# An attention and mixture-of-experts block on one core: the last ten tiles' residual, LayerNorm 2 steps and low rows on VectorE, the last six tiles' router work in three PSUM banks

## The reference

```
h = layernorm(x) * (1 + ca) + sa
x = x + ga * attention(h)        # 16 heads, 16 segments of 64 tokens, causal inside a segment,
                                 # a memory M, z per head carried from segment to segment
h = layernorm(x) * (1 + cb) + sb
logits = h @ router_w.T          # 8 experts, 2 per token
x = x + gb * (weighted sum of the two chosen experts' silu(gate) * up @ w2)
```

## Time and profile before

| | us |
|---|---|
| median of three runs | 1365.4 |
| lowest and highest of them | 1361.44 and 1370.28 |
| the profiled execution | 1369.37 |
| its span, first to last instruction | 1367.3 |
| DVE busy in it | 939.0 (69%) |
| POOL busy | 927.2 (68%) |
| PE busy | 1192.2 (87%) |
| ACT busy | 706.6 (52%) |

### The profile page before, as it was taken

One profiled execution on the slowest core, in us unless ns is written; L12 is line 12 of the kernel. 1 busy time (PEld: TensorE's weight loads), 2 busy tenths in 40 slices (PEclk: granted clock), 3 DMA queues, 4 the chain that ended last, 5 costly groups with the idle time before them and its releaser, 6 DMA issues. The chain is left out here.

```text
span 1367.3 us, 54718 instructions
## 1 busy us (share of the span) xinstructions
PE 1192.2 (87%) x20142; PEld 1016.3 (74%) x20142; DVE 939.0 (69%) x2509; ACT 706.6 (52%) x1391; POOL 927.2 (68%) x989
## 2 busy tenths in 40 slices
PE   3499999999889998989613899999999999999995
PEld 0277778787767777767413699999999999999994
DVE  2389889998888998878668655555555555555552
ACT  2267878887878887877632222323322232322321
POOL 3158989998988898888910466666666666666643
PEclk8599999999999999999855999999999999999998
DMA  9811333334443434443461454545455455555540
GB/s 225 175 55 51 76 91 94 91 96 109 110 97 88 104 104 99 109 99 97 112 216 16 105 99 91 98 92 98 91 101 101 92 95 95 98 94 98 99 75 1
DMA packets 124476, 134.54 MB, mean 98 GB/s; under 512 B 26090, under 2 KB 103986, under 8 KB 124098
## 3 DMA queue, kind: packets, MB, share of 16 engines
q0 software_dynamic: 32592, 56.77, 22.0%
q1 hardware_dynamic: 89762, 67.46, 20.1%
q10 hardware_dynamic: 1872, 6.82, 1.8%
HBM read 63.60 MB, written 44.04 MB: 79 GB/s over the span
## 5 line engine op out<-in xcount | busy, mean ns | idle before, releaser
L1131 PE MATMUL psum<-xT,xall 128*128 128x256 f16 x3408 | 396.6, 273 | 2.5 <-DVE xT L1118 0.9
L1131 PEld LDWEIGHTS psum<-xT,xall 128*128 x3408 | 331.1, 98 | 40.9 <-issue 3.2
L1191 POOL DMA_INDIRECT out<-yo,sidx x142 | 226.4, 1594 | 198.4 <-DVE yo L1182 172.1
L1139 ACT ACTIVATE sg<-psum 128x512 f32<-128x512 f32 x142 | 84.7, 597 | 317.6 <-PE psum L1131 282.8
L1144 DVE SCALAR_TENSOR_TENSOR hf<-psum,sg 128x512 f32<-128x512 f32 x142 | 98.2, 691 | 209.2 <-ACT sg L1139 205.3
L1101 POOL DMA_INDIRECT grow<-moe_rows,gidx x142 | 142.6, 1004 | 99.5 <-DVE sidx L992 56.5
L1165 PE MATMUL psum<-w2s,hT 128*128 x1704 | 197.7, 273 | 2.6 <-DVE w2s L1217 2.4
L1165 PEld LDWEIGHTS psum<-w2s,hT 128*128 128x128 f16 x1704 | 166.5, 98 | 22.5 <-issue 3.2
L1151 ACT ACTIVATE hT<-hf 128x512 f16<-128x512 f32 x142 | 89.5, 630 | 111.4 <-DVE hf L1144 104.6
L569 POOL TENSOR_TENSOR pT<-sc,pT 128x1024 f16<-128x1024 f32 x64 | 136.5, 2133 | 10.1 <-ACT pT L565 10.1
L1155 DVE TENSOR_TENSOR hT<-hf,hT 128x512 f16<-128x512 f32 x142 | 98.3, 692 | 57.0 <-ACT hT L1151 40.4
(11 more groups left out here) (217 smaller groups left out, 2429.9 us busy)
## 6 DMA issues: line engine op xcount, KB each, us to landing
stk<-qk SPq DMA_DIRECT2D x384, 64.0 KB
moe_rows<-hrows SPq DMA_DIRECT2D x128, 128.0 KB, 2.4
out<-xall SPq DMA_DIRECT2D x128, 64.0 KB, 2.1
xall<-in_x SPq DMA_DIRECT2D x8, 896.0 KB, 18.1
raw<-in_w ACTq DMA_DIRECT2D x13, 512.0 KB, 5.5
raw<-in_w SPq DMA_DIRECT2D x8, 512.0 KB, 7.9
grow<-moe_rows,gidx POOLq DMA_INDIRECT x142
out<-yo,sidx POOLq DMA_INDIRECT x142
```

Source lines behind the costliest of these rows:

```text
L1131: i = k.e.matmul(bank[:, n * LONG:(n + 1) * LONG], w13s[:, bass.ds(ex_reg * (G * 4 * I) + ((2 * c + b_) * 2 * I + col), P)], xT[:, k.b, a, ...
L1139: done(k.e.activation(sg[:, half, :], bGate[half][:, :], ACT.Silu, scale=1.0 / W_SCALE), "sg")
L1191: k.e.indirect_dma_start(out_rows, bass.IndirectOffsetOnAxis(ap=sidx[:, n:n + 1], axis=0), yo[:, k.v, q, :], None, bounds_check=B * T - 1, ...
```

## The change

The four elementwise stages `res_add`, `ln2_mult`, `ln2_add` and `rows_lo` run on VectorE, instead of on GpSimd, for tiles 54 to 63 (LATE = 54). They have semaphores of their own, and `when` directs whoever waits for such a tile to them. For tiles 58 to 63 (END = 58) the router's transposes alternate between bank C (odd tiles) and bank H (even tiles), and the logits go to bank B. Banks B and C are otherwise used by the projections and by `update`, so these tiles also wait until `update_dve` of the last tile is done.

```
+LATE = NT - 10
+END = NT - 6
...
-    bkAh, bkDh, bkHh = bkA.bitcast(F16), bkD.bitcast(F16), bkH.bitcast(F16)
+    bkAh, bkCh, bkDh, bkHh = [bank.bitcast(F16) for bank in (bkA, bkC, bkD, bkH)]
...
+    LATE_ON_VECTOR = ("res", "l2a", "l2b", "hlo")
+    S_late = {n: sem("a_late_" + n) for n in LATE_ON_VECTOR}
...
+            if of >= LATE and stage in LATE_ON_VECTOR:
+                return S_late[stage], of - LATE + 1
...
+    def done_late(ins, stage):
+        ins.then_inc(S_late[stage], 1)
...
     def res_add(k):
-        k.wait("gat")
-        done(k.e.tensor_tensor(k.of_tile(xall), k.of_tile(xall), gat[:, k.b, :], ALU.add), "res")
+        if k.t < LATE:
+            k.wait("gat")
+            done(k.e.tensor_tensor(k.of_tile(xall), k.of_tile(xall), gat[:, k.b, :], ALU.add), "res")
+    def res_add_late(k):
+        if k.t >= LATE:
+            k.wait("gat")
+            done_late(k.e.tensor_tensor(k.of_tile(xall), k.of_tile(xall), gat[:, k.b, :], ALU.add), "res")
...
     def ln2_mult(k):
-        k.wait("xn2")
-        done(k.e.tensor_tensor(h2[:, k.b, :], h2[:, k.b, :], mods[:, mCB, k.j, :], ALU.mult), "l2a")
+        if k.t < LATE:
+            k.wait("xn2")
+            done(k.e.tensor_tensor(h2[:, k.b, :], h2[:, k.b, :], mods[:, mCB, k.j, :], ALU.mult), "l2a")
     def ln2_add(k):
-        k.wait("l2a")
-        done(k.e.tensor_tensor(h2[:, k.b, :], h2[:, k.b, :], mods[:, mB2, k.j, :], ALU.add), "l2b")
+        if k.t < LATE:
+            k.wait("l2a")
+            done(k.e.tensor_tensor(h2[:, k.b, :], h2[:, k.b, :], mods[:, mB2, k.j, :], ALU.add), "l2b")
...
+    def ln2_mult_late(k):
+        if k.t >= LATE:
+            k.wait("xn2")
+            done_late(k.e.tensor_tensor(h2[:, k.b, :], h2[:, k.b, :], mods[:, mCB, k.j, :], ALU.mult), "l2a")
+    def ln2_add_late(k):
+        if k.t >= LATE:
+            k.wait("l2a")
+            done_late(k.e.tensor_tensor(h2[:, k.b, :], h2[:, k.b, :], mods[:, mB2, k.j, :], ALU.add), "l2b")
...
     def rows_lo(k):
-        k.wait("hhi")
-        done(k.e.tensor_tensor(hrows[:, k.j, D:2 * D], h2[:, k.b, :], hrows[:, k.j, 0:D], ALU.subtract), "hlo")
+        if k.t < LATE:
+            k.wait("hhi")
+            done(k.e.tensor_tensor(hrows[:, k.j, D:2 * D], h2[:, k.b, :], hrows[:, k.j, 0:D], ALU.subtract), "hlo")
+    def rows_lo_late(k):
+        if k.t >= LATE:
+            k.wait("hhi")
+            done_late(k.e.tensor_tensor(hrows[:, k.j, D:2 * D], h2[:, k.b, :], hrows[:, k.j, 0:D], ALU.subtract), "hlo")
...
+    def h2_bank(k):
+        return bkCh if k.t >= END and k.t % 2 else bkHh
     def h2_trans(k):
         k.wait("hhi")
         k.wait("hlo")
-        k.wait_banks("h2Tr")
+        if h2_bank(k) is bkCh:
+            k.e.wait_ge(S["umul"], NT)
+            k.wait("h2T", 2)
+        elif k.t >= END + 2:
+            k.wait("h2T", 2)
+            k.wait("gat", -4)
+        else:
+            k.wait_banks("h2Tr")
         for n in range(2 * G):
-            i = k.e.transpose(bkHh[:, n * P:(n + 1) * P], hrows[:, k.j, n * P:(n + 1) * P], idh[:, :])
+            i = k.e.transpose(h2_bank(k)[:, n * P:(n + 1) * P], hrows[:, k.j, n * P:(n + 1) * P], idh[:, :])
...
         k.wait("rtr", 2)
-        done(k.e.activation(h2T[:, k.b, :, :, :].rearrange("p a c t -> p (a c t)"), bkHh[:, 0:2 * D], ACT.Copy), "h2T")
+        done(k.e.activation(h2T[:, k.b, :, :, :].rearrange("p a c t -> p (a c t)"), h2_bank(k)[:, 0:2 * D], ACT.Copy), "h2T")
+    def logit_bank(k):
+        return bkB if k.t >= END else bkH
     def router(k):
         k.wait("h2T")
-        k.wait_banks("rtr")
+        if k.t >= END:
+            k.e.wait_ge(S["umul"], NT)
+            k.wait("lg", 1)
+        else:
+            k.wait_banks("rtr")
         for c in range(G):
             for a, b_ in PARTS:
-                i = k.e.matmul(bkH[:, D:D + E], h2T[:, k.b, a, c, :], rws[:, b_, c, :],
+                i = k.e.matmul(logit_bank(k)[:, D:D + E], h2T[:, k.b, a, c, :], rws[:, b_, c, :],
                                start=(c == 0 and (a, b_) == PARTS[0]), stop=(c == G - 1 and (a, b_) == PARTS[-1]))
         done(i, "rtr")
     def logit_copy(k):
         k.wait("rtr")
-        done(k.e.activation(logits[:, :, k.t], bkH[:, D:D + E], ACT.Copy,
+        done(k.e.activation(logits[:, :, k.t], logit_bank(k)[:, D:D + E], ACT.Copy,
                                scale=1.0 / W_SCALE), "lg")
...
         "vector": [(2, aggr), (9, mem_a), (9, mem_v), (0, stats), (9, v_rest), (9, v_new), (11, pv_den),
-                  (11, pv_scale), (11, pv_dve), (14, ln2_shift), (8, q_rest), (8, sigma), (13, resid),
-                  (9, row_max), (10, update_dve), (13, stats2), (7, h1t_rest), (8, mem_den), (9, max_rest),
-                  (13, aggr2), (8, mem_rec), (13, var_eps2)],
+                  (11, pv_scale), (11, pv_dve), (14, ln2_shift), (16, rows_lo_late), (8, q_rest), (8, sigma), (13, resid),
+                  (9, row_max), (10, update_dve), (13, res_add_late), (13, stats2), (7, h1t_rest), (8, mem_den), (9, max_rest),
+                  (13, aggr2), (8, mem_rec), (13, var_eps2),
+                  (15, ln2_mult_late), (15, ln2_add_late)],
```

## The result

| | before | changed kernel |
|---|---|---|
| median of 20 runs each, us | 1361.98 | 1372.23 |
| lowest and highest | 1355.77, 1370.28 | 1366.46, 1381.80 |
| span of the profiled execution | 1367.3 | 1373.0 |
| `resid` of tile 54 to the next block, in the profile | 86.46 | 98.07 |

The ratio is 1.0071, with a 95% interval from 1.0051 to 1.009: slower, by less than 1%. The three runs shown ahead of the prediction had a median 3.4 us above that of all 20, so 1372 against 1362 is the pair to compare: +10.3 us where the sum said +12.0.

The account below looks back on a forecast made before the run. VectorE and GpSimd were taken as full first, GpSimd alone from tile 60. Delays of 12.5 us at tile 63 less 0.55 gave +12.0 on 1369.4, 1381.3; less 4.0 to the median, 1377 us, range 1362 to 1386.

Parts of the forecast that it names:

- the sum: Attention stage: 12.5 us delay at `resid` of tile 63 less 0.55 in the stage's end gives +12.0 us.
- the relief rival: Tiles 60 to 63: taking 2.8 us a round off full POOL (GpSimd) pays first; -4 us, 1361, chance 0.13.
- VectorE sets the pace: Up to tile 60: moved instructions add 1.6 us a round of own time, plus waits; `resid` of tile 60 +9.7 us.
- Turns: Moved two-SBUF-input instructions on VectorE wait for GpSimd's running instruction: 1.35 us a round, from 0 to 2.5.
- The stall at `v_rest`: VectorE waits for ScalarE's `v_high`, queued behind `rows_hi`, which waits for the LayerNorm pair: 0.6 us, tiles 56 and 57.
- Tile 59 to 60: Stretch between these residuals: 3.0 us added less 2.2 us that VectorE was free; running delay from +8.9 to +9.7.
- The clock: Stretches from tile 58 on: TensorE's clock falls earlier, slowing `pv`, `scores`, `w_o`; +18 us, 1383; clock and more 0.17.
- The ring: From tile 60 on: chain from `resid` over VectorE's pair, ScalarE and `w_o` to the next `resid`, 6.2 us.
- Tile 60 to 61: Stretch of 7.67 us before: 6.2 us plus 1.2 for the pair meeting `p_rest` of tile 63, 7.4, so -0.3.
- No turns: Moved 128x256 instructions on VectorE do not wait for POOL: about 7.5 us less, +4.5, 1370, chance 0.20.
- The tail: From `resid` of tile 63 to the next block: stores end it, 13.3 us against 13.85, -0.55.
- the bank edit itself I cost at 0: Stage's end: the three banks' gain is covered by the stores; without that cover it would bring 2.6 us.

Follow-up runs that it names:

- the one-operand kernel: Changed kernel with each of the four late instructions replaced by statistics over one SBUF tile, against the kernel before: ratio 1.0041 (1.0005 to 1.0077).
- the banks-only kernel: Kernel before with the three banks alone, all four elementwise steps staying on GpSimd: ratio 0.9998, 1363.31 us.
- the two from tile 60 on: Changed kernel with the four steps on VectorE for tiles 60 to 63 only, in its own or the early VectorE order, against before: 1.0024 and 0.9987.
- the early places: Changed kernel with low rows, pair and residual earlier in VectorE's list, against before: 1.0091 for all ten tiles, 0.9987 for the last four.

## Why the prediction was right, step by step

The direction, the mechanism and the size were right, but the closeness of the sum is in part luck. By the table, the sum and the profile differ by 0.4 us at the stage's end and by up to 1.15 us in single stretches, with both signs: the stretches of tiles 56 to 58 were taken 0.8 and 1.1 us too long, those of tiles 59 to 61 1.15 and 1.0 too short. The range was 24 us wide and held "no change" (1365.4), so lying in it says little; and 1361, the price of the relief rival, lies outside it, against what the prediction says of its lower end.

*VectorE sets the pace (right).* Stretch of tile 56 to 57: own work 1.6, turns 0.40 + 0.50 (residual and low rows, by their durations), stall 0.62, less the 0.3 that VectorE was free: 2.8, measured 2.76 (11.17 - 8.41). Stretch of 57 to 58: 1.6 + 0.28 + 0.58 less the 1.76 of the wait for `scores` and 0.3: 0.4, measured 0.40. Stretch of 58 to 59: 1.6 + 1.0 + 0.5, less 0.25 as the weight rounding no longer waits (1.22 at 659.34, for the 1.47 of the earlier trace rows) and 0.25 of VectorE's gaps: 2.6, measured 2.60. The own times and the stall hold, with the turns put in as they came; the prediction itself left out the 0.3 us that VectorE was free in the first of these stretches.

*Turns (right in kind, too large).* The prediction took 0.6 for the residual, 0.3 for the pair and 0.45 for the low rows, 1.35 a round, and 1.2 at the last `p_rest`: 7.9 us over five rounds (it wrote "about 7.5"). The ten tiles show 0.5 on average for the first six residuals (0.94 for that of tile 55, most of why tile 56 is late by 1.6 and not 1.1), nothing for the pair but the 1.17 at `p_rest` of tile 63, and 0.5, 0.28, 0.5 and 0 for the low rows: 5.2 us in their durations, 4.4 at the stage's end by the one-operand kernel. The step that was mis-sized is "for the pair 0.3, near half of a 0.7 instruction": at the end of VectorE's round GpSimd is idle and waits for VectorE's own `var_eps2`, since the moved work is what used to fill it (idle 1.29, 2.22 and 1.95 us there, then the inverse root, in the rounds of tiles 56 to 58).

*The stall at `v_rest` (right).* Predicted 0.6, measured 0.62 and 0.58, and gone in every kernel in which the pair isn't at the end of these rounds.

*Tile 59 to 60 (wrong, and it evened the sum out).* Predicted +0.8, measured +1.95 (8.90 - 6.95), with 2.2 us of VectorE idle: not VectorE's doing. TensorE's clock was 0.73. The banks-only kernel has 8.68 us there at 0.68, the two from tile 60 on 8.34 at 0.71 and 9.01 at 0.51. In the profile of before the clock fell a stretch later; all nine experiments and the changed kernel show it by this stretch (0.51 to 0.73). Part of it comes back in the next stretch (6.97 for 7.67 in the banks-only kernel), and at tile 63 that kernel is 1.3 us late. So I estimate that about 1.3 us of the measured 11.6 belong to the one profile of before and not to the change; 10.3 are left, and the medians differ by 10.3. A second profile of before would show it, and there is none.

*The clock (the rival, +18).* Half of its mechanism came: the clock fell to 0.66 for tiles 58 to 59. Its price didn't: VectorE, not TensorE, was last there, and the 2.60 us of that stretch are accounted for without it. In this profile it costs where VectorE has room, in one stretch.

*The ring (right, 0.25 to 0.55 long).* Predicted 6.2, measured 5.96 and 5.65. The 0.3 for turns of the pair is again what was too much, and in the second `a_high` has no tile left, for which the 5.96 have 0.31 (685.41 to 685.72). Tile 60 to 61 was predicted at 7.4 and took 8.40; the meeting with the last `p_rest` was as taken (1.17 for 1.2). The rest stands in ScalarE's timeline of the changed kernel:

```profile
677.71 0.42 ACT L772 ACTIVATE hrows<-h 128x256 f16<-128x256 f32 x1 [2.41 <-DVE h L767]
...
678.50 1.05 ACT L69 ACTIVATE xall<-raw 128x1024 f16<-128x1024 f32 x1
...
679.45 0.41 ACT L691 ACTIVATE ah<-att_o 128x256 f16<-128x256 f32 x1
679.75 0.59 ACT L707 ACTIVATE aT<-psum 128x512 f16<-128x512 f16 x1
```

The weight rounding `w13_high` (L69) of this round stands between `rows_hi` and `a_act`, 2.04 us from start to start where the ring above has 1.11. And `update_dve` stands once more between `resid` and the residual: 2.12 us from `resid` to the pair for 1.80. So 5.96 + 1.17 + 0.93 + 0.32 = 8.38 of the 8.40; the prediction had both instructions at nothing here.

*POOL's relief (the rival on the other side, -4).* Out: GpSimd's list did get short, but no stretch between residuals did. The ring over VectorE and ScalarE is 5.7 to 6.0, where the rival needed under 4.7. Its premise, which the sum shares ("here POOL was the bound"), fails too for the last two stretches. Busy time by stretch with the early places, tiles 61 to 62 for all ten tiles and 62 to 63 for the last four:

```profile
673.16:677.98 4.82, 2.77 (x20) 1.75 (x20) 4.39 (x11) 2.50 (x6) 2.10 (x2) 0.50 0.11 26
...
677.90:682.42 4.52, 2.78 (x20) 1.76 (x20) 2.92 (x11) 2.14 (x5) 0.66 (x1) 0.50 0.30 65
```

GpSimd is busy 2.10 and 0.66 us there, for 4.82 and 4.06 in the earlier trace rows, and the stretches are 4.82 and 4.52 all the same. In the shorter one the chain over TensorE and ScalarE stands at the same offsets in both kernels: `router`, `logit_copy`, `h2_trans`, `h2_act`, `a_act` and `w_o` start 0.53, 0.86, 1.25, 1.87, 2.37 and 3.02 us behind `resid` of tile 62 in before, and 0.52, 0.86, 1.25, 1.88, 2.37 and 3.02 here. In the longer one, with `a_high` in it, the offsets agree within 0.01 us as well (`w_o` at 3.32 in both). That chain, not GpSimd, sets those rounds.

*No turns (+4.5).* Out by the rows above. The one-operand kernel, which is that rival made real, lost 7.2 us in the stage, 5.9 without the 1.3 of the clock: by that estimate the rival's own price was 1.4 too low.

*The tail (right in sum, wrong in its cause).* Predicted 13.3, measured 13.19. But the step "the bank edit itself I cost at 0: it is covered by the stores" failed: in before the logits, not the stores, were last, by 0.8 us, and behind the moved instructions they would have been later still. The edit alone brings 0.8 us, with the moved instructions 1.8. The last issue's end came 11.17 us behind `resid`, for 11.6, and the block's end 2.02 behind that, for 1.7.

## What to carry to other kernels

In these traces, moving elementwise work with two SBUF inputs from GpSimd to VectorE cost its own time on VectorE plus the wait behind whatever GpSimd was in at that place, however short the moved instruction was; look up, for each place in the list, what GpSimd runs then, the longest instruction above all. GpSimd being full is no reason to relieve it: for six of the ten tiles VectorE was as full, and in the last rounds another chain set the pace. And where a moved step releases a third engine, write the ring out, step by step, with every instruction that stands in it in that round: it gave the new length within 0.25 to 0.55 us where that was done, and was 1.0 short where two instructions were left out.

## What was not expected of the hardware

TensorE's granted clock falls near the end of the attention stage, and in kernels with the same instructions up to tile 60 it doesn't fall in the same stretch: from tile 59 to 60 it is 1.00 in before, 0.68 with only the bank edit, 0.71 and 0.51 in the two kernels that move from tile 60 on, and in these last two it is 0.89 and 0.92 already one stretch earlier. From 6.95 to 8.68 us this stretch moves by 1.7, more than the whole effect of the bank edit. It shows why one profile's stretches must be held against a second kernel that is equal up to there.

A VectorE addition of eight columns took 1.52 us, over nine times its own 0.16, without any idle time in the trace.
